# Run-in of the L2 attention heads: other spare products on TensorE

## The chip, the cores and the metric

The kernel runs on one core of a Trainium2 chip. The metric is the time of one execution on the device in microseconds (us); lower is better. Half a per cent of it is about 9.7 us.

## The reference, cut to what matters

A sequence of 2 x 1024 tokens with 256 features passes four layers, all in float32: L0 (cumulative-sum attention and a feed-forward), L1 (single-head attention and a feed-forward), L2 (16-head attention with heads of 16 features) and L3 (16 heads of 64 features, then an expert stage). The change touches the heads of L2 only:

```python
h = _sln(hidden, w, ln_g, ln_b, Wg, bg, Wb, bb)
qkv = (h @ Wqkv.T + bqkv).reshape(B, N, num_heads, hd, 3)
q = jnp.moveaxis(qkv[..., 0], 2, 1)
k = jnp.moveaxis(qkv[..., 1], 2, 1)
v = jnp.moveaxis(qkv[..., 2], 2, 1)
energy = jnp.einsum('bhqd,bhkd->bhqk', q, k)
att = jax.nn.softmax(energy, axis=-1) / D ** 0.5
out = jnp.einsum('bhqk,bhkd->bhqd', att, v)
```

With B = 2 and 16 heads there are 32 maps of 1024 x 1024 scores with an inner size of 16.

## The kernel before

The layers run one after the other as stages; a barrier of all engines stands between two. The stage of the L2 heads is `NarrowPairs`. It takes the 32 heads in 16 pairs; the two heads of a pair sit in the two halves of the 128 rows of the TensorE array (rows 0 to 63 and rows 64 to 127). Queries and keys are split into a high and a low part of the type fp32r and stacked, so that one product with 48 rows gives the three cross terms.

Scores are computed twice. First by query rows (`row`, L1756): two products of 48 x 128 weights and 512 columns fill a PSUM tile `rowb` of 128 x 1024 for each head, and VectorE takes the row maximum of it (L1824, tile `l2h_nm`). The maxima of a pair are turned and placed as two more rows of the stacked queries (the DMAs of `place_shift`). Then by keys (`score`, L1772): 50-row products give the shifted scores, already transposed; ScalarE takes the exponent (L1874, into `pT`), and `mix` (L1786) multiplies by the values. A mix uses all 128 rows and 32 columns of the array, four side by side. Its operands are plain float32, and each such product shows as two records in the trace.

`pe_program` is one hand-written order: for turns m = -2 to 16, steps k = 0 to 7, phases 0 and 1. In each phase come two `row` products of one head, each followed by a `score` product of the pair m on the other half of the array, and then `mix` products of two steps before. `ahead` says which rows are due: those of pair m + 1 (k below 4) or m + 2, so row maxima run twelve steps ahead of the scores. In the turns m below 0 there are no scores yet: the 12 steps with rows (8 of pair 0, 4 of pair 1), 24 phases, are the **run-in**. In it `ahead_of_scores` (L1763) puts spare products where the scores will stand later: 48 rows, 512 columns, in the half of the array that `row` does not use, into a `score` tile that nobody reads. Nothing waits for them, and they wait for nothing.

`row` waits with its first product for the maximum taken before from the same `rowb` half (semaphore `maxes`); VectorE waits for `rowsums`. Steps 0 and 1 of pair 0 (m = 0) have no mix, since a mix comes two steps behind. At the end of the stage `pe_out` (L2336) puts some ordinary float32 products of 128 x 128 weights and 256 columns between the last scores; they belong to the output projection.

Of the kernel before, what the change touches and what calls it, by code (L numbers as in the profile page):

```python
# [22 lines left out]
P = 128  # L23
# [4 lines left out]
C = 512  # L28
# [10 lines left out]
class Semaphores:  # L39


    def __init__(self, nc):
        self.nc, self.held = nc, []
# [1597 lines left out]
class NarrowPairs:  # L1641
# [8 lines left out]
    OUT = 5  # L1650

    def __init__(self, s, parts, V, out, ident, hd, vscale, tiles, pending, later):
        self.V, (self.out, self.sums), self.hd, self.vscale = V, out, hd, vscale
        self.mw = 32
        (self.K, self.Q), self.pending = tiles, pending
        self.Q = self.Q + [s.sb("Q3", [P, S], F32R)]
        self.vs = s.sb("vs", [P, self.SLOTS, 2, TB, self.mw])
        self.pT = s.sb("pT", [P, 4, 2, S])
        self.osb = s.sb("osb", [P, 2, C])
        self.nm = s.sb("nm", [P, 2, 2 * TB])  # L1660
        self.parts_nm = s.sb("nm_parts", [P, 4 * TB], F32R)
        self.shift = s.sb("shift", [P, 4 * TB])
        self.rowb = [s.ps(f"rowb{i}", (P, S)) for i in range(2)]
        self.score = [s.ps(f"score{i}") for i in range(3)]
        self.ob = s.ps("out")
        self.loaded = [s.sem(f"loaded{i}") for i in range(self.SLOTS)]
        self.stored = [s.sem(f"stored{i}") for i in range(2)]
        (self.constants, self.staged, self.rowsums, self.maxes, self.high, self.split, self.turned, self.shifted,
         self.scores, self.exps, self.mixed, self.ocopied) = (s.sem(n) for n in (
             "v_constants", "v_staged", "row_scores", "maxima", "maxima_hi", "maxima_lo", "maxima_turned",  # L1670
             "shift_in_stack", "scores", "exps", "mixed", "out_copied"))
        self.q, self.k = parts
        self.second_load, self.last_store, self.second_pair = later
# [73 lines left out]
    def pe_program(self, pe):  # L1747
        def row(m, t, h, c):
            u, r = m % self.SLOTS, 64 * h
            if c == 0:  # L1750
                if t == 0:
                    self.need(pe, self.loaded[u], (m // self.SLOTS + (u >= self.EARLY)) * 16 * self.LOADS)
                    if m == 1:
                        pe.wait_ge(self.second_pair, 16 * self.LOADS)
                self.need(pe, self.maxes, (TB * m + t) * 2 + h - 1)
            mm = pe.matmul(self.rowb[h][:, c * C:(c + 1) * C], self.Q[u][r:r + self.SPLIT, t * P:(t + 1) * P],  # L1756
                           self.K[u][r:r + self.SPLIT, c * C:(c + 1) * C], start=True, stop=True)
            if c == 1:
                mm.then_inc(self.rowsums, 1)

        def ahead_of_scores(t, h, c):
            r = 64 * h
            pe.matmul(self.score[2 - 2 * h][:, :], self.Q[0][r:r + self.SPLIT, t * P:(t + 1) * P],  # L1763
                      self.K[0][r:r + self.SPLIT, c * C:(c + 1) * C], start=True, stop=True)

        def score(m, k, h, c, place):
            u, r = m % self.SLOTS, 64 * h
            v = 4 * (TB * m + k) + place
            if k == 0 and place == 0:
                pe.wait_ge(self.shifted, 8 * 16 * (m + 1))  # L1770
            self.need(pe, self.exps, v - 2)
            pe.matmul(self.score[v % 3][:, :], self.K[u][r:r + self.SPLIT + 2, k * P:(k + 1) * P],  # L1772
                      self.Q[u][r:r + self.SPLIT + 2, c * C:(c + 1) * C], start=True, stop=True).then_inc(self.scores, 1)

        def mix(m, k, part):
            g = TB * m + k
            if part == 0:
                pe.wait_ge(self.exps, 4 * (g + 1))
            if k == 0 and part == 0:
                pe.wait_ge(self.staged, m + 1)  # L1780
                self.need(pe, self.ocopied, m)
            at, w = (part * C // 2, C // 2) if 0 < k < TB - 1 else (0, C)
            for h in range(2):
                for c in range(2):
                    r = self.mw * (2 * h + c)
                    mm = pe.matmul(self.ob[r:r + self.mw, at:at + w], self.vs[:, m % self.SLOTS, h, k, :],  # L1786
                                   self.pT[:, g % 4, h, c * C + at:c * C + at + w], start=k == 0, stop=k == TB - 1)
            if at + w == C:
                mm.then_inc(self.mixed, 1)

        for m in self.TURNS:
            for k in range(TB):
                mr, tr = self.ahead(m, k)
                for phase in range(2):
                    for c in range(2):
                        if self.there(mr):
                            row(mr, tr, phase, c)
                        if self.there(m):
                            score(m, k, *self.part(mr, phase, c))
                        elif m < 0 and self.there(mr):  # L1800
                            ahead_of_scores(tr, 1 - phase, c)
                    mine, kk = (m, k - self.LAG) if k >= self.LAG else (m - 1, k - self.LAG + TB)
                    if self.there(mine) and (phase == 0 or 0 < kk < TB - 1):
                        mix(mine, kk, phase)
                step = TB * (m - self.N + 2) + k - self.OUT
                if step == 0:
                    pe.wait_ge(self.maxes, 2 * TB * self.N)
                if 0 <= step < 2:
                    self.tokens.pe_out(pe, 0, self.rowb[0], 2 * step, 2 * step + 2)
                elif 2 <= step < 6:  # L1810
                    self.tokens.pe_out(pe, 1, self.rowb[1], step - 2, step - 1)
# [1481 lines left out]
```

## Time and profile before

| | us |
|---|---|
| median of 3 runs | 1941.92 (1938.81 to 1947.23) |
| the profiled execution | 1945.03 |
| its span on the core | 1943.3 |
| TensorE busy (share of the span) | 1768.1 (91%) |
| VectorE busy | 1471.1 (76%) |
| ScalarE busy | 1142.5 (59%) |
| GpSimd busy | 815.7 (42%) |

The heads of L2 run from 510.7 to about 882 us. A timeline row has its start, its length, engine, line, operation and tiles; rows of one kind that follow each other are merged (x2, x8), and lengths of neighbours on PE overlap, so the time that a product takes from the engine is read as the distance between starts. PE is the matmul, PEld the load of its weights. PEclk is the granted TensorE clock as a share of full speed: 0.50 is 1.2 GHz, 1.00 is 2.4 GHz.

### The profile page before, as it was taken

How to read it: one execution, taken by the hardware profiler on the slowest of the kernel's cores; microseconds unless marked ns; L12 is line 12 of the kernel's file. 1: busy time of each engine (PE TensorE's matmuls, PEld its weight loads, DVE VectorE, ACT ScalarE, POOL GpSimd, SP SyncE). 2: the span in 40 equal slices, each digit the busy share in tenths (PEclk: the TensorE clock that was granted, in tenths of full speed). 3: DMA queues.
4: the chain of work that ended last, by engine and by line, in shares of the span. 5: the costliest groups of instructions: out<-in, count | busy, mean ns of one | idle time of the engine just before them, and what ended most of it. 6: DMA issues, size and time to landing. Idle time of an engine off the chain costs nothing. (4 is left out here: it accounts for less than half of the span.)

```text
span 1943.3 us, 37413 instructions
## 1 busy us (share of the span) xinstructions
PE 1768.1 (91%) x14461; PEld 1169.6 (60%) x14461; DVE 1471.1 (76%) x2454; ACT 1142.5 (59%) x2029; POOL 815.7 (42%) x738
## 2 busy tenths in 40 slices
PE   7998999898799999998989599999999999882896
PEld 5766589697533333346767465566666666671885
DVE  5666745745779999986987688888888888467794
ACT  3332333533158888875567577777777777332663
POOL 3465620464130411002655545544555555105576
PEclk9999999999669999999999899999999999995888
DMA  5000000201523212213669854555456553308352
GB/s 161 1 1 28 1 14 1 66 1 45 187 60 98 59 41 54 53 30 120 203 203 281 218 120 107 120 124 117 113 124 160 143 141 88 109 12 252 95 141 44
DMA packets 196193, 191.28 MB, mean 98 GB/s; under 512 B 64496, under 2 KB 154352, under 8 KB 195760
## 3 DMA queue, kind: packets, MB, share of 16 engines
q1 hardware_dynamic: 192944, 184.69, 35.6%
q0 software_dynamic: 3072, 4.20, 1.2%
q8 instruction: 115, 1.88, 0.4%
q14 instruction: 62, 0.51, 0.1%
HBM read 121.20 MB, written 67.37 MB: 97 GB/s over the span
## 5 line engine op out<-in xcount | busy, mean ns | idle before, releaser
L1624 POOL TENSOR_SCALAR l3h_prob<-l3h_prob,l3h_inv 128x1024 f32<-128x1024 f32 x256 | 284.4, 1124 | 283.6 <-DVE l3h_inv L1584 283.6
L1824 DVE TENSOR_REDUCE l2h_nm<-l2h_rowb 128x1 f32<-128x1024 f32 x256 | 302.6, 1218 | 29.1 <-PE l2h_rowb L1756 28.7
L1577 DVE TENSOR_REDUCE l3h_nmax<-l3h_score 128x1 f32<-128x1024 f32 x256 | 309.6, 1215 | 12.1 <-PE l3h_score L1514 8.2
L1874 ACT ACTIVATE l2h_pT<-l2h_score 128x512 f32<-128x512 f32 x512 | 273.9, 597 | 51.2 <-PE l2h_score L1772 31.8
L1607 ACT ACTIVATE l3h_prob<-l3h_score,l3h_nmax 128x1024 f32<-128x1024 f32 x256 | 282.5, 1113 | 2.9 <-DVE l3h_nmax L1577 2.7
L1569 DVE COPY l3h_pT<-l3h_ring 128x512 f32<-128x512 f32 x256 | 176.2, 688 | 95.5 <-PE l3h_ring L1527 95.5
L1539 PE MATMUL l3h_out<-l3h_pT,l3h_vs 128*64 128x512 f32 x1024 | 247.3, 605 | 0.8 <-ACT l3h_osb L1600 0.8
L1571 ACT ACTIVATE l3h_pT<-l3h_ring 128x512 f32<-128x512 f32 x256 | 154.2, 602 | 138.8 <-PE l3h_ring L1527 138.8
L1527 PEld LDWEIGHTS l3h_ring<-ident,l3h_prob 64*128 64x128 f32 x4096 | 157.2, 138 | 129.0 <-POOL l3h_prob L1624 111.6
L1527 PE MATMUL l3h_ring<-ident,l3h_prob 64*128 64x64 f32 x4096 | 175.3, 225 | 9.7 <-POOL l3h_prob L1624 8.0
L1786 PE MATMUL l2h_out<-l2h_pT,l2h_vs 128*32 128x256 f32 (+1 forms) x1792 | 160.1, 431 | 0.0
L2701 POOL TENSOR_TENSOR l3qkv_lo<-l3qkv_full,l3qkv_hi 128x1024 fp32r<-128x1024 f32 x32 | 97.9, 3063 | 95.0 <-ACT l3qkv_hi L2598 95.0
L1756 PE MATMUL l2h_rowb<-l2K,l2Q 48*128 48x512 f32 x256 | 103.6, 502 | 11.5 <-PEq L69 7.7
L1514 PE MATMUL l3h_score<-k3first,q3first 64*128 64x512 f32 x768 | 106.6, 409 | 7.7 <-PEq L69 6.1
L1539 PEld LDWEIGHTS l3h_out<-l3h_pT,l3h_vs 128*64 128x64 f32 x1024 | 62.6, 136 | 84.6 <-issue 76.2
L1514 PE MATMUL l3h_score<-l3h_K,l3h_Q 64*128 64x512 f32 x768 | 105.7, 405 | 0.4
L1772 PE MATMUL l2h_score<-l2Q,l2K 50*128 50x512 f32 x256 | 99.3, 472 | 1.1 <-ACT l2h_pT L1874 0.5
L1299 POOL TENSOR_TENSOR l1mlp_y_lo<-l1mlp_y,l1mlp_y_hi 128x512 fp32r<-128x512 f32 x32 | 44.6, 1418 | 125.3 <-DVE l1mlp_y_hi L1411 125.3
L1756 PEld LDWEIGHTS l2h_rowb<-l2K,l2Q 48*128 48x128 f32 x256 | 45.3, 216 | 72.7 <-DVE l2h_nm L1824 57.6
L1786 PEld LDWEIGHTS l2h_out<-l2h_pT,l2h_vs 128*32 128x32 f32 x1792 | 35.9, 109 | 77.1 <-issue 47.5
L1514 PEld LDWEIGHTS l3h_score<-k3first,q3first 64*128 64x128 f32 x768 | 68.3, 188 | 20.8 <-issue 6.3
L1514 PEld LDWEIGHTS l3h_score<-l3h_K,l3h_Q 64*128 64x128 f32 x768 | 67.4, 186 | 13.1 <-ACT l3h_prob L1607 1.8
(484 smaller groups left out, 4288.8 us busy)
## 6 DMA issues: line engine op xcount, KB each, us to landing
q3first<-l_q SPq DMA_DIRECT2D x64, 256.0 KB, 4.3
l3h_Q<-l_q SPq DMA_DIRECT2D x64, 256.0 KB, 4.2
l_q<-l3qkv_hi SPq DMA_DIRECT2D x16, 512.0 KB, 5.0
l_q<-l3qkv_lo SPq DMA_DIRECT2D x16, 512.0 KB, 4.6
l_k<-l3qkv_hi SPq DMA_DIRECT2D x16, 512.0 KB, 4.3
l_k<-l3qkv_lo SPq DMA_DIRECT2D x16, 512.0 KB, 3.4
k3first<-l_k SPq DMA_DIRECT2D x64, 128.0 KB, 4.5
l3h_vs<-l_v SPq DMA_DIRECT2D x32, 256.0 KB, 2.8
```

Source lines behind the costliest of these rows:

```text
L1514: mm = pe.matmul(self.score[t % 2][:, c * C:(c + 1) * C], self.Q[u][r, x, t * P:(t + 1) * P], self.K[u][r, y, :], start=i == 0, stop=i == 2)
L1527: mm = pe.transpose(self.turn_bank(g, half)[:, kk * P // 2:(kk + 1) * P // 2], self.prob[r, g % 4, kk * P:(kk + 1) * P], self.ident[r, r])
L1539: mm = pe.matmul(self.ob[c * self.hd:(c + 1) * self.hd, :], self.vs[:, n % 2, kk, :], self.pT[:, n % 2, kk, c * C:(c + 1) * C], start=kk = ...
L1569: eng.tensor_copy(dst, src).then_inc(self.emptied_d, 1)
L1571: eng.activation(dst, src, ACT.Copy).then_inc(self.emptied_a, 1)
L1577: dve.tensor_reduce(self.nmax[:, g % 4:g % 4 + 1], self.score[g % 2][:, :], AX.X, ALU.max, negate=True).then_inc(self.maxes, 1)
L1607: act.activation(self.prob[:, q, :], self.score[g % 2][:, :], ACT.Exp, bias=self.nmax[:, q:q + 1], accum_out=self.total[:, q:q + 1]).then_ ...
L1624: pool.tensor_scalar(self.prob[:, q, :], self.prob[:, q, :], self.inv[:, q:q + 1], self.vscale, ALU.mult, ALU.mult).then_inc(self.scaled, 1)
L1756: mm = pe.matmul(self.rowb[h][:, c * C:(c + 1) * C], self.Q[u][r:r + self.SPLIT, t * P:(t + 1) * P], self.K[u][r:r + self.SPLIT, c * C:(c ...
L1786: mm = pe.matmul(self.ob[r:r + self.mw, at:at + w], self.vs[:, m % self.SLOTS, h, k, :], self.pT[:, g % 4, h, c * C + at:c * C + at + w], ...
L1824: dve.tensor_reduce(self.nm[:, mr % 2, at:at + 1], self.rowb[h][:, :], AX.X, ALU.max, negate=True).then_inc(self.maxes, 1)
L1874: act.activation(self.pT[:, g % 4, h, c * C:(c + 1) * C], self.score[v % 3][:, :], ACT.Exp).then_inc(self.exps, 1)
```

## The change

The spare products of the run-in are others. `ahead_of_scores` goes, and `spare` comes: the identity (128 x 128, float32) as weights, 256 columns of the tokens `X` as the moving operand, into the first 256 columns of `score[0]` and `score[1]`. They use all 128 rows and all 128 columns of the array, and plain float32 in place of fp32r. There were four spare products in a step, one after each `row` product; there are still four, but two behind each pair of `row` products. So the number stays at 48. The results are read by nobody, as before.

```diff
-        def ahead_of_scores(t, h, c):
-            r = 64 * h
-            pe.matmul(self.score[2 - 2 * h][:, :], self.Q[0][r:r + self.SPLIT, t * P:(t + 1) * P],
-                      self.K[0][r:r + self.SPLIT, c * C:(c + 1) * C], start=True, stop=True)
+        def spare(i):
+            pe.matmul(self.score[i][:, 0:2 * P], self.ident[:, :], self.tokens.X[:, i, :],
+                      start=True, stop=True)
@@
                             row(mr, tr, phase, c)
                         if self.there(m):
                             score(m, k, *self.part(mr, phase, c))
-                        elif m < 0 and self.there(mr):
-                            ahead_of_scores(tr, 1 - phase, c)
+                    if m < 0 and self.there(mr):
+                        for i in range(2):
+                            spare(i)
```

On TensorE (PE), at the start of the stage of the L2 heads, the order before is this (`l2h_rowb` is written by `row`, `l2h_score` by the spare products; one row of before is one product):

```order
L69 UNCONDITIONAL_BRANCH
L2062 UNCONDITIONAL_BRANCH
L1756 MATMUL l2h_rowb<-l2K,l2Q 128x512
L1763 MATMUL l2h_score<-l2K,l2Q 128x512
L1756 MATMUL l2h_rowb<-l2K,l2Q 128x512
L1763 MATMUL l2h_score<-l2K,l2Q 128x512
L1756 MATMUL l2h_rowb<-l2K,l2Q 128x512
L1763 MATMUL l2h_score<-l2K,l2Q 128x512
```

And this is what stands on the same engine at the same place with the change (x2 are two products in a row):

```order
L69 UNCONDITIONAL_BRANCH
L2062 UNCONDITIONAL_BRANCH
L1756 MATMUL l2h_rowb<-l2K,l2Q 128x512 x2
L1762 MATMUL l2h_score<-X,ident 128x256 x2
L1756 MATMUL l2h_rowb<-l2K,l2Q 128x512 x2
L1762 MATMUL l2h_score<-X,ident 128x256 x2
```

Row products of one half of the array no longer have a neighbour for the other half; each two of them are followed by two products that take the whole array. The other engines' instructions are the same, in the same order.

## Rows read from the trace of the kernel before

**Rows 1.** Page: busy share in 40 slices of the span, and the granted clock.

```profile
PE   7998999898799999998989599999999999882896
...
DVE  5666745745779999986987688888888888467794
...
PEclk9999999999669999999999899999999999995888
```

**Rows 2.** Stretches: us, busy and count of PE, PEld, DVE, ACT, POOL; PEclk; DMA share; GB/s.

```profile
511.00:541.00 30.00, 27.40 (x96) 12.09 (x96) 27.14 (x26) 0.00 (x0) 3.55 (x12) 0.50 0.66 201
547.00:566.00 19.00, 18.80 (x101) 6.54 (x100) 12.05 (x14) 10.15 (x20) 8.65 (x8) 0.50 0.01 1
570.00:575.00 5.00, 5.00 (x50) 1.94 (x43) 4.65 (x4) 4.39 (x10) 3.54 (x3) 1.00 0.82 152
```

**Rows 3.** Timeline of the run-in: its first product, one phase, the first real score.

```profile
510.76 0.76 PE L1756 MATMUL l2h_rowb<-l2K,l2Q 48*128 48x512 f32 x1 [7.73 <-PEq L69]
...
538.98 0.79 PE L1756 MATMUL l2h_rowb<-l2K,l2Q 48*128 48x512 f32 x1 [0.18 <-DVE l2h_nm L1824]
538.98 0.28 PEld L1763 LDWEIGHTS l2h_score<-l2K,l2Q 48*128 48x128 f32 x1
538.98 0.79 PE L1763 MATMUL l2h_score<-l2K,l2Q 48*128 48x512 f32 x1
...
540.24 2.36 DVE L1824 TENSOR_REDUCE l2h_nm<-l2h_rowb 128x1 f32<-128x1024 f32 x2 [0.17 <-PE l2h_rowb L1756]
...
541.52 0.79 PE L1772 MATMUL l2h_score<-l2Q,l2K 50*128 50x512 f32 x1
```

**Rows 4.** Timeline of PE: one phase at half clock, then the start of the next.

```profile
560.04 0.79 PE L1772 MATMUL l2h_score<-l2Q,l2K 50*128 50x512 f32 x1
560.63 0.62 PE L1756 MATMUL l2h_rowb<-q3first,k3first 48*128 48x512 f32 x1
...
561.19 1.08 PE L1786 MATMUL l2h_out<-l2h_pT,l2h_vs 128*32 128x256 f32 x8
562.20 0.79 PE L1756 MATMUL l2h_rowb<-q3first,k3first 48*128 48x512 f32 x1
```

**Rows 5.** Timeline of PE: the same at full clock.

```profile
588.69 0.64 PE L1786 MATMUL l2h_out<-l2h_pT,l2h_vs 128*32 128x256 f32 x8
589.26 0.49 PE L1756 MATMUL l2h_rowb<-q3first,l2h_Q 48*128 48x512 f32 x1
...
589.92 0.64 PE L1786 MATMUL l2h_out<-l2h_pT,l2h_vs 128*32 128x256 f32 x8
```

**Rows 6.** Timeline of PE at full clock: whole-array float32 products between half-array scores.

```profile
865.65 0.50 PE L1772 MATMUL l2h_score<-l2h_Q,q3first 50*128 50x512 f32 x2
866.08 1.13 PE L2336 MATMUL l2h_rowb<-carry,V 128*128 128x256 f32 x4
867.14 0.51 PE L1772 MATMUL l2h_score<-l2h_Q,q3first 50*128 50x512 f32 x2
```

**Rows 7.** Weight loads of whole-array float32 products of 512 columns at half clock.

```profile
466.05 0.34 PEld L2002 LDWEIGHTS l2qkv_bank<-l2qkv_norm_out,carry 128*128 128x128 f32 x1 [0.52 <-issue]
466.90 0.34 PEld L2002 LDWEIGHTS l2qkv_bank<-l2qkv_norm_out,carry 128*128 128x128 f32 x1 [0.52 <-issue]
```

**Rows 8.** VectorE once in each pair, behind the pair's last row maximum (pairs 1 to 3).

```profile
556.07 0.17 DVE L1831 CAST l2h_nm_parts<-l2h_nm 128x16 fp32r<-128x16 f32 x1
581.32 0.17 DVE L1831 CAST l2h_nm_parts<-l2h_nm 128x16 fp32r<-128x16 f32 x1
601.58 0.17 DVE L1831 CAST l2h_nm_parts<-l2h_nm 128x16 fp32r<-128x16 f32 x1
```

**Rows 9.** Stretches in which the clock rises, stays or falls elsewhere (columns as in Rows 2).

```profile
463.00:464.00 1.00, 0.54 (x3) 0.57 (x4) 0.97 (x5) 1.00 (x2) 0.00 (x0) 0.50 0.00 0
...
467.00:468.00 1.00, 1.00 (x3) 0.49 (x2) 0.00 (x0) 1.00 (x2) 1.00 (x1) 0.74 0.00 0
...
501.50:505.00 3.50, 1.53 (x13) 1.33 (x12) 2.28 (x5) 0.00 (x0) 0.00 (x0) 1.00 0.72 148
505.00:506.00 1.00, 0.00 (x0) 0.00 (x0) 0.00 (x0) 0.00 (x0) 0.00 (x0) 0.53 0.53 195
```

More of the change, by code:

```diff
@@ L1652, in __init__ @@
     def __init__(self, s, parts, V, out, ident, hd, vscale, tiles, pending, later):
-        self.V, (self.out, self.sums), self.hd, self.vscale = V, out, hd, vscale
+        self.V, (self.out, self.sums), self.ident, self.hd, self.vscale = V, out, ident, hd, vscale
         self.mw = 32
```

## The prediction

> **What bounds the kernel now.** I read the page's slices first. TensorE is busy nearly everywhere, but in slices 11 and 12 the granted clock falls to 0.6 [rows 1]. Those slices hold the start of the L2 heads, so next I read the stretches there. From 511 to 541 us, the run-in, PEclk is 0.50 (1.2 GHz), PE is busy 27.40 of 30 us and VectorE 27.14 of 30; from 547 to 566 us PE is busy 18.80 of 19 us and the clock is still 0.50; from 570 us it is 1.00 [rows 2]. Thus the place has two parts with different limits:
>
> In the run-in **VectorE** sets the pace in spite of the slow clock. A pair of row maxima takes 2.36 us, VectorE waits only 0.17 us before it, and the next row product waits for the maximum [rows 3]. The run-in lasts from 510.76 to 541.52 us: 30.76 us for 24 phases, 1.28 us a phase.
>
> Behind it **TensorE at half clock** sets the pace. A phase there is 1.15 us of row and score products and 1.01 us of mixes, 2.16 us (560.04 to 561.19 to 562.20) [rows 4]; at full clock it is 0.66 us (589.26 to 589.92) and 0.57 us (588.69 to 589.26) [rows 5].
>
> What the slow clock costs: a pair in steady state takes 601.58 - 581.32 = 20.26 us. From one such mark (behind the fourth step's maxima) to the next, the one before takes 581.32 - 556.07 = 25.25 us, 5.0 more [rows 8]. For the part before 556.07 us: the mark lies four steps behind the first score, 556.07 - 541.52 = 14.5 us; four steps are half of 20.26, and the mark comes about 1 us after them (the last maximum has to wait for its product), which makes 11.1 us in steady state. That is 3.4 us more. Together **8.4 us**: all that a perfect clock behind the run-in could give back. Of it I take 7.5, since the exponent table is still loaded by ScalarE at the first score.
>
> **The change, part by part.**
>
> *Removed:* 48 half-array spare products. Each ran in the other half of the array beside a row product, with the same start, 538.98 us [rows 3]. They took no time of their own: worth 0.
>
> *Added:* 48 whole-array float32 products, two in each phase. They can't run beside row products, for they need the rows of both halves. A float32 product of 512 columns is two records, and at half clock one follows the other by 0.85 us (466.05 to 466.90) [rows 7]; at 256 columns I take half, 0.43 us, so two products, four records, are 1.71 us. Passing from half-array to whole-array products and back has a price: at full clock four records stand between scores for 867.14 - 866.08 = 1.06 us [rows 6], 0.86 us of it streaming by half of 0.43 each, and 0.20 us the change-over. At half clock the mixes show a change-over of 1.01 - 0.86 = 0.15 us [rows 4] against 0.57 - 0.43 = 0.14 us at full [rows 5], so it grows little; I take 0.25 us. Bounds: 0.15 and 0.35.
>
> The row products alone: each two follow each other in the same half, as now; 1.15 us at half clock [rows 4], 0.66 us at full [rows 5]. I don't expect them to be quicker without a neighbour in the other half. Lower bounds are 1.00 and 0.43 us, if the change-over is counted only once (a pair of scores before the whole-array products takes 866.08 - 865.65 = 0.43 us [rows 6]).
>
> So a phase of the run-in is
>
> - at half clock 1.15 + 1.71 + 0.25 = **3.11 us** (2.86 to 3.2), against 1.28 now;
> - at full clock 0.66 + 1.06 = **1.72 us** (1.29 to 1.72), against 1.28 now.
>
> Either way TensorE becomes the bound of the run-in and VectorE, with 1.2 us of work a phase, waits. The cover that hid spare work (the other half of the array) is gone, and the four products a step lie on the path. Nothing else moves: no wait is added, the queues of the other engines hold the same instructions, and the loads of later pairs only get more time.
>
> The Trainium skill says the same of the change-over: "TensorEngine Tiling (Array Packing)", section "Key Properties", has a switch of the tiling mode drain the engine. By that rule each phase pays two drains that the present spare products, of the same mode as the rows, don't pay. The trace agrees, with the 0.20 us above.
>
> **Does the clock rise?** This decides the size. For it: whole-array products with little else bring it up within about 4 us (PE idle in part of 463 to 464 us, 0.74 in 467 to 468 us) [rows 9]. Against it: from 547 to 566 us TensorE is busy 99% [rows 2], 47% of it with mixes on all rows and columns and 53% with products on 96 to 98 rows [rows 4], and yet the clock stays at 0.50 for 19 us. In the new run-in the whole-array products hold 1.96 of 3.11 us, 63%, but the remaining 37% are row products on 48 of 128 rows with nothing beside them. By rows in use times streaming time, the new mix has 1.71 + 0.375 x 0.85 = 2.03 us in 3.11, or 0.65; the stretch that stayed cold has 0.86 + 0.77 x 0.86 = 1.52 us in 2.16, or 0.70; the present run-in has 0.77 x 0.86 in 1.28, or 0.51. So the new run-in is more active than the old one, but no more than a stretch that stayed slow for 19 us. I take it that the clock stays low through the run-in, with little certainty.
>
> **Sum of the forecast (case A).** 24 x 3.11 = 74.6 us in place of 30.8: +43.9 us (68.6 to 76.8 by the bounds: +38 to +46). Behind the run-in the same slow stretch of about 19 us as now follows, as the products there are unchanged: 0, give or take 5. The profiled execution would go from 1945.0 to 1989; it lies 3.1 us above the median, and from the median 1941.9 it is **1986 us**, own range 1979 to 1993.
>
> **Rivals.**
>
> *B, the clock rises early and stays.* Two phases at half clock, the rest full: 24 x 1.72 + 2 x 1.39 = 44.1 us, +13.3; the 7.5 us behind it are won: +5.8, 1948 us. The skill's page "TensorE: Matmul & The Clock Gate", Part 1, speaks for a rise: there the throttled clock is the default state and sustained matmul activity releases it. The rows at 467 us agree with it; those at 547 to 566 us don't, busy as the engine is.
>
> *C, it rises early and falls again.* In steps 0 and 1 of pair 0 there are no mixes, and at full clock the engine has 0.66 us of half-array work in each 1.28 us. At 501.5 to 505 us it was busy 1.53 of 3.5 us and the clock fell [rows 9]. Then most of the 7.5 us are lost again: +12, 1954 us.
>
> *D, it rises late,* after some twelve phases: 10.6 + 12 x 1.39 - 7.5 = +19.8, 1962 us.
>
> *E, not slower.* The clock rises at once and the change-overs are hidden, so that a phase at full clock is 0.43 + 0.86 = 1.29 us, and VectorE stays the bound. The run-in then grows by 3.4 us only (two phases at 2.86, the rest 0.01 each), and 7.5 are won: -4, 1938 us. It decides where a phase at full clock falls below 1.45 us, since 24 x 0.17 + 3.4 = 7.5. The 1.06 us of rows 6 speaks against it. Even without any cost the gain would end at 8.4 us, below half a per cent.
>
> **How the numbers follow.** A 0.50, B 0.20, C 0.13, D 0.12, E 0.03, others 0.02. About 0.5% (9.7 us) can be told from no change here. A, C and D are slower by more: 0.75; B and E within it: 0.23; faster by more: 0.02. The predicted time is A's, 1986 us. B must be partly in the range, since A, C and D alone hold 0.75: 1947 to 1993 us.
>
> **What would show it.** In the timeline of the changed kernel the first real score (now at 541.52 us) should come at about 585 us, with PEclk 0.50 in all stretches before, four records of the identity product 0.43 us apart in each phase, and VectorE idle near 1.9 us before each maximum. If PEclk is 1.00 from some point on, the phases from there are to be 1.72 us long, and the case is B, C or D by when it rises and whether 541 to 548 us' counterpart keeps it. I am wrong in the sizing if a phase at half clock is not near 3.1 us, and wrong in the main step if the clock rises among row products on 48 rows.

## The result

The changed kernel takes 1986.2 us (median of 6 executions, 1982.78 to 1990.55), the kernel before 1946.3 us (6 executions, 1938.81 to 1951.84). The ratio is 1.0206 with a 95% interval of 1.0182 to 1.0230: 2% slower, 40 us. The median of the kernel before is now 4.4 us above the 1941.9 of the forecast, which came from its first three executions. The profiled execution of the changed kernel has a span of 1988.8 us, against 1943.3.

The answers to [rows 1] are these lines of the page after: the busy share in 40 slices and the granted clock, each slice now 49.7 us.

```profile
PE   7998999899899999998989789999999999892886
...
DVE  6676646656347999996888688888888888556896
...
PEclk9999999999557999999999899999999999995798
```

TensorE is busier than before in slices 11 and 12 (89 where there was 79), VectorE less (34 where there was 77), and the clock in them went from 66 to 55, with a 7 in the slice behind. More work, no more speed.

The stretches of the changed kernel that answer to [rows 2] (us, busy and count of PE, PEld, DVE, ACT, POOL; PEclk; DMA share; GB/s):

```profile
509.00:584.00 75.00, 75.00 (x144) 39.89 (x144) 29.95 (x27) 0.00 (x0) 3.54 (x12) 0.50 0.32 89
584.40:622.50 38.10, 37.12 (x189) 14.02 (x188) 23.34 (x22) 21.51 (x39) 15.96 (x12) 0.50 0.09 22
625.00:630.00 5.00, 4.99 (x44) 1.84 (x40) 4.64 (x5) 4.18 (x9) 0.00 (x0) 1.00 0.11 25
```

The run-in is over 75 us long now. PE is busy in all of the first stretch, VectorE in 30 of its 75 us, and the clock is 0.50 throughout. The bound has gone from VectorE to TensorE. The timeline of the run-in's end, answering to [rows 3]:

```profile
579.27 2.07 PE L1762 MATMUL l2h_score<-X,ident 128*128 128x256 f32 x4
579.38 1.23 DVE L1824 TENSOR_REDUCE l2h_nm<-l2h_rowb 128x1 f32<-128x1024 f32 x1 [1.93 <-PE l2h_rowb L1756]
...
581.27 1.22 PE L1756 MATMUL l2h_rowb<-l2K,l2Q 48*128 48x512 f32 x2
...
582.42 2.07 PE L1762 MATMUL l2h_score<-X,ident 128*128 128x256 f32 x4
...
584.43 0.79 PE L1771 MATMUL l2h_score<-l2Q,l2K 50*128 50x512 f32 x1
```

One phase is 1.15 us of row products (581.27 to 582.42) and 2.01 us of spare ones (582.42 to 584.43), 3.16 us in all, and VectorE waits 1.93 us before its maximum where it had waited 0.17 for a pair of them. The first row product comes at 508.77 us, the first real score at 584.43: 75.7 us for 24 phases, 44.9 more than before.

Behind it the slow stretch is a little longer than it was. The marks of [rows 8] are now at

```profile
598.99 0.17 DVE L1831 CAST l2h_nm_parts<-l2h_nm 128x16 fp32r<-128x16 f32 x1
630.04 0.17 DVE L1831 CAST l2h_nm_parts<-l2h_nm 128x16 fp32r<-128x16 f32 x1
650.34 0.17 DVE L1831 CAST l2h_nm_parts<-l2h_nm 128x16 fp32r<-128x16 f32 x1
```

and 630.04 - 584.43 = 45.6 us from the first score to the second of them, against 581.32 - 541.52 = 39.8. The last pair has the steady 20.3 us. The balance of the profiled executions: start of the stage 2.0 us earlier, run-in +44.9, slow stretch +5.8, the rest of the program about -3, span +45.5. The medians are 40 us apart; a single execution of either kernel lies some microseconds off, and the profiled one of the changed kernel was the longest of its six.

### The profile page after: what moved, and what is told of

Same layout as the page of the kernel before. It is cut to its first block and busy times, and to the rows that moved or that the text cites. A ratio compares the mean times of both kernels' runs of the same rounds, so it can differ in the third digit from the quotient of the medians.

```text
span 1988.8 us, 37509 instructions
## 1 busy us (share of the span) xinstructions
PE 1818.5 (91%) x14509; PEld 1200.7 (60%) x14509; DVE 1475.0 (74%) x2454; ACT 1141.3 (57%) x2029; POOL 809.7 (41%) x738
## 5 line engine op out<-in xcount | busy, mean ns | idle before, releaser
L1514 PEld LDWEIGHTS l3h_score<-l3h_K,l3h_Q 64*128 64x128 f32 x768 | 68.0, 186 | 12.8 <-ACT l3h_prob L1607 1.8
```

Source lines behind the costliest of these rows:

```text
L1514: mm = pe.matmul(self.score[t % 2][:, c * C:(c + 1) * C], self.Q[u][r, x, t * P:(t + 1) * P], self.K[u][r, y, :], start=i == 0, stop=i == 2)
```

## The experiments

Each kernel is told by its difference to the kernel before or the changed one. Only spare products differ. A time without a number of executions is that of a single one. In one of the comparisons below, 23 executions of the kernel before reached from 1931.5 to 1954.9 us around a median of 1945.6, so a single time can be off by some 10 us, and the readings rest on the traces. "Theory" and "rival" are those of the expectation shown.

**Spare products taken away.** Of before, without the two lines that call `ahead_of_scores`:

```diff
-                        elif m < 0 and self.there(mr):
-                            ahead_of_scores(tr, 1 - phase, c)
```

> The run-in without any spare product: only the two row products of each phase are left on TensorE. The changed kernel's extra time is put down to spare products that have the array to themselves; the spare products of before ran beside the rows and should have cost nothing. Theory: VectorE still sets the pace, 24 phases of 1.28 us, first row product to first real score 30.8 us, PEclk 0.50, total as before, 1942 to 1947 us. Rival (the spare products of before already did something for the clock): the slow stretch behind the run-in gets longer than 25 us by over 10 us, total 1950 or more.

Measured: 1951.9 us, beside 1954.2 for the kernel before on the same chip. The run-in's stretch:

```profile
511.00:541.00 30.00, 26.30 (x49) 10.94 (x45) 27.66 (x27) 0.00 (x0) 3.03 (x11) 0.50 0.68 200
```

And two pairs of maxima in its timeline:

```profile
537.18 2.36 DVE L1822 TENSOR_REDUCE l2h_nm<-l2h_rowb 128x1 f32<-128x1024 f32 x2 [0.18 <-PE l2h_rowb L1756]
...
539.72 2.36 DVE L1822 TENSOR_REDUCE l2h_nm<-l2h_rowb 128x1 f32<-128x1024 f32 x2 [0.18 <-PE l2h_rowb L1756]
```

VectorE's pairs of maxima are 2.54 us apart (537.18 to 539.72), two phases of 1.27 us: as with the spare products. These had cost no time in a phase, and the clock came back 25 us after the first score with them and without. The first score itself came later than expected, 32.8 us after the first row product (510.25 to 543.01) and not 30.8: it waited 1.22 us for the transfer of the shifts. Whether that is chance of this one execution isn't shown.

**One whole-array product a phase.** Of the changed kernel:

```diff
                     if m < 0 and self.there(mr):
-                        for i in range(2):
-                            spare(i)
+                        spare(phase)
```

> One whole-array spare product in each phase in place of two. Theory (streaming of the product, 0.43 us a record at half clock, carries the cost, and a change-over of about 0.3 us is paid once a phase): a phase of 1.15 + 0.86 + 0.29 = 2.30 us at PEclk 0.50, run-in 55 us against 75.7 with two, total about 1966 us. Rival (the change between half-array and whole-array products carries the cost, whatever the number): a phase of 2.9 us or more, total 1980.

Measured: 1969.8 us. The timeline of PE:

```profile
540.05 1.22 PE L1756 MATMUL l2h_rowb<-l2K,l2Q 48*128 48x512 f32 x2
541.20 1.22 PE L1762 MATMUL l2h_score<-X,ident 128*128 128x256 f32 x2
542.35 1.22 PE L1756 MATMUL l2h_rowb<-l2K,l2Q 48*128 48x512 f32 x2
```

A phase is 2.30 us, 0.85 less than with two. The product costs its streaming, two records of 0.43 us. The theory holds for the phase and for the run-in (55.2 us), and the total lies 4 us above its 1966 us; the rival (2.9 us whatever the number) is out.

**Two more change-overs a phase.** Of the changed kernel, the same 48 products in another order:

```diff
                             score(m, k, *self.part(mr, phase, c))
-                    if m < 0 and self.there(mr):
-                        for i in range(2):
-                            spare(i)
+                        elif m < 0 and self.there(mr):
+                            spare(c)
```

> The changed kernel with its two spare products of a phase placed one behind each row product instead of both behind the second: the same 48 products, but two changes more in a phase between half-array and whole-array products. It measures the change-over by itself. Theory (about 0.3 us for a change there and back at half clock): a phase of 3.15 + 0.3 = 3.45 us, run-in 83 us, total about 7 us above the changed kernel. Rival (the change-over costs nothing, the rest of the 3.15 us is weight loading of the products themselves): 3.15 us a phase.

Measured: 1995.3 us, and a timeline of PE of

```profile
538.32 0.79 PE L1756 MATMUL l2h_rowb<-l2K,l2Q 48*128 48x512 f32 x1
539.04 1.22 PE L1762 MATMUL l2h_score<-X,ident 128*128 128x256 f32 x2
540.19 0.79 PE L1756 MATMUL l2h_rowb<-l2K,l2Q 48*128 48x512 f32 x1
540.91 1.22 PE L1762 MATMUL l2h_score<-X,ident 128*128 128x256 f32 x2
542.06 0.79 PE L1756 MATMUL l2h_rowb<-l2K,l2Q 48*128 48x512 f32 x1
```

A phase is 3.74 us (538.32 to 542.06), not the 3.45 expected: two changes more cost 0.59 us, so **one change is 0.29 us at half clock**, in either direction. A row product alone takes 0.72 us, 0.43 of it streaming; a spare product 1.15 us, 0.86 of it streaming. With that the changed kernel's phase comes out: 4 x 0.43 + 2 x 0.43 + 2 x 0.29 = 3.16 us. I had put the way into the whole-array products too low, at 0.25 us in the prediction, and in the expectation I had put both ways together at 0.3 us. The run-in grew by 14 us against the changed kernel, the total by 9 against its median: the clock came back 10 us after the first score here and 38 us after it there.

**Both kinds of spare products.** Of the changed kernel, with `ahead_of_scores` put back beside the rows (called `beside`):

```diff
                         if self.there(m):
                             score(m, k, *self.part(mr, phase, c))
+                        elif m < 0 and self.there(mr):
+                            beside(tr, 1 - phase, c)
                     if m < 0 and self.there(mr):
                         for i in range(2):
                             spare(i)
```

> The changed kernel with the half-array spare products of before put back beside the row products, in addition to the two whole-array ones. Theory (the clock stays low because the row products leave over half of the array idle for 1.15 of 3.15 us): the first phases take 3.15 us, as now, then PEclk goes to 1.00 within the run-in, and phases take 1.72 us; run-in 42 to 60 us, total 1950 to 1970. Rival (products with the identity as weights, nearly all zeros, don't count for the clock): PEclk 0.50 for all of the run-in, 3.15 us a phase, total 1986.

Measured: 1959.5 us. Stretches:

```profile
513.00:528.00 15.00, 15.00 (x40) 8.23 (x40) 6.12 (x5) 0.00 (x0) 2.60 (x10) 0.50 0.63 199
530.00:561.00 31.00, 31.00 (x145) 17.55 (x144) 22.14 (x22) 0.00 (x0) 0.00 (x0) 1.00 0.38 103
561.00:567.00 6.00, 4.66 (x22) 2.30 (x20) 5.01 (x5) 5.23 (x10) 0.00 (x0) 1.00 0.00 0
568.00:570.00 2.00, 2.00 (x12) 0.83 (x6) 0.25 (x1) 0.23 (x2) 0.00 (x0) 0.50 0.00 0
```

This is the run that tells most, and the theory holds. The products added take no time of their own (3.15 us a phase at half clock, 514.98 to 518.13), yet the clock rises within the run-in, near 529 us, and from then on a phase is

```profile
531.84 0.50 PE L1756 MATMUL l2h_rowb<-l2K,l2Q 48*128 48x512 f32 x1
...
532.51 1.13 PE L1762 MATMUL l2h_score<-X,ident 128*128 128x256 f32 x4
533.57 0.50 PE L1756 MATMUL l2h_rowb<-l2K,l2Q 48*128 48x512 f32 x1
```

1.73 us long, 0.67 and 1.06. So the clock stayed low in the changed kernel although PE was busy 75 of 75 us, and what it lacked was the products beside the rows, in the other half of the array. Behind the first score, in the steps without mixes, the clock falls again, but only from 567.0 to 570.5 us. To see whether the rise is regular, the same kernel was timed:

> The kernel with both kinds of spare products again, now timed: whether the clock rises within the run-in every time or did so once. Theory: in every execution it rises somewhere in the run-in, the total lies between 1945 and 1972 us by when, the clock of each execution is above the 0.93 of the changed kernel. Rival (it was chance): some executions at 1984 to 1991 us with 0.93.

Measured: 1955.0 us median of 10 executions (1945.25 to 1961.95), ratio to before 1.0048 (1.0026 to 1.0071). The clock of the executions is 0.945 to 0.956; with the changed kernel it is 0.929 to 0.934 in all six. By these clocks and times it rises each time; two of the eleven executions were profiled and show it. In the new profile it rose at about 515 us, in the second phase:

```profile
514.00:515.00 1.00, 1.00 (x5) 0.35 (x5) 0.00 (x0) 0.00 (x0) 0.37 (x2) 0.50 1.04 193
515.00:516.00 1.00, 1.00 (x4) 0.79 (x4) 0.98 (x1) 0.00 (x0) 0.00 (x0) 0.77 0.95 201
516.00:517.00 1.00, 1.00 (x7) 0.41 (x6) 0.26 (x2) 0.00 (x0) 0.00 (x0) 1.00 0.68 70
```

Even so the kernel is no faster than before. The run-in takes 43.6 us (510.61 to 554.16), 12.8 more than before, and from the first score to the second of the marks of [rows 8] (here at 587.16 us) it takes 33.0 us against 39.8, 6.8 less: a run-in of 1.73 us a phase costs more than the clock gives back.

**Other weights.** Of the changed kernel:

```diff
-            pe.matmul(self.score[i][:, 0:2 * P], self.ident[:, :], self.tokens.X[:, i, :],
+            pe.matmul(self.score[i][:, 0:2 * P], self.tokens.X[:, 2 + i, 0:P], self.tokens.X[:, i, :],
```

> The changed kernel with 128 columns of the tokens as weights of the spare products in place of the identity, so that nearly all weights are other than zero. Theory (the weights' values don't matter; it is the half-array rows without a neighbour): 3.15 us a phase, PEclk 0.50 through the run-in, total 1980 to 1991. Rival (zeros in the weights kept the clock low): it rises within the run-in, total below 1972.

Measured: 1983.0 us, PEclk 0.50 through the run-in, and on PE

```profile
540.70 1.22 PE L1756 MATMUL l2h_rowb<-l2K,l2Q 48*128 48x512 f32 x2
541.85 2.07 PE L1762 MATMUL l2h_score<-X 128*128 128x256 f32 x4
543.85 1.22 PE L1756 MATMUL l2h_rowb<-l2K,l2Q 48*128 48x512 f32 x2
```

a phase of 3.15 us. The theory holds: the zeros of the identity are not what kept the clock low.

**Starting with a full clock.** Of the changed kernel, 14 products at the end of TensorE's program of the stage before, in the time in which it waits for the barrier:

```diff
+            for i in range(14):
+                pe.matmul(bank[0][:, 0:2 * P], g["ident"][:, :], X[:, i % 2, :], start=True, stop=True)
```

> The changed kernel with 14 more identity products at the end of the stage before, in the 7 us in which TensorE waits for the barrier, so that the run-in starts at full clock. Theory: at PEclk 1.00 a phase takes 0.66 + 1.06 = 1.72 us, the run-in 41 us if the clock holds; total 1944 to 1956 by whether the clock also holds in the two steps without mixes. Rival (the clock falls in the run-in even when it starts full): phases go back to 3.15 us, total 1975 to 1986.

Measured: 1993.0 us. The theory fell. The rival has the phase right; the time lies above its 1975 to 1986 us. PE's timeline, and two stretches of it:

```profile
503.47 6.21 PE L2024 MATMUL l2qkv_bank<-X,ident 128*128 128x256 f32 x28
511.20 0.69 PE L1756 MATMUL l2h_rowb<-l2K,l2Q 48*128 48x512 f32 x2 [1.53 <-PEq L69]
511.82 1.26 PE L1762 MATMUL l2h_score<-X,ident 128*128 128x256 f32 x4
513.01 1.22 PE L1756 MATMUL l2h_rowb<-l2K,l2Q 48*128 48x512 f32 x2
```

```profile
512.00:513.00 1.00, 1.00 (x4) 0.50 (x4) 1.00 (x1) 0.00 (x0) 1.00 (x3) 0.85 0.66 236
513.00:514.00 1.00, 1.00 (x3) 0.50 (x2) 0.16 (x1) 0.00 (x0) 1.00 (x6) 0.50 0.69 223
```

The stage starts at full clock, but PE had stood still for 1.5 us at the barrier, and within the first phase the clock falls. From 515 to 580 us it is 0.50 with PE busy 65 of 65 us. So once low, it did not come back in a run-in of this make, here and in the changed kernel. Whether the standstill or the row products without neighbours took it down, this run doesn't tell apart.

The same 14 products ahead of the run-in of the kernel before:

> The kernel before with 14 whole-array products in the wait for the barrier ahead of the stage, and its own half-array spare products in the run-in. In the two-product run-in that began full the clock fell after the first phase; here the row products have a neighbour in the other half, but at full clock TensorE would be busy with them only 0.66 of 1.28 us. Theory: PEclk is 1.00 for the first microseconds and falls to 0.50 within about 5 us, total as before (within 5 us). Rival (half-array pairs keep a clock that is already full): PEclk 1.00 up to the first real score and behind it, the slow stretch is gone, 7 to 8 us faster than before.

Measured: 1947.8 us. PEclk is 0.92 from 511 to 512 us and 0.50 from 512 to 540; it comes back at about 566 us, as in the kernel before. The theory holds, no gain. Here too PE had stood still at the barrier, for 2.09 us, so the run doesn't show that half-array pairs alone lose a full clock.

**Keeping it.** Three kernels tried to beat both. The first has the 14 products, `beside`, and one whole-array product a phase:

```diff
+                        elif m < 0 and self.there(mr):
+                            beside(tr, 1 - phase, c)
                     if m < 0 and self.there(mr):
-                        for i in range(2):
-                            spare(i)
+                        spare(phase)
```

> Three things at once: 14 products in the wait for the barrier, half-array spare products beside the rows, one whole-array spare product a phase. Theory: PEclk 1.00 from the start of the run-in to its end, a phase of 0.66 + 0.64 = 1.30 us, run-in 31 to 32 us; then in the two steps without mixes the clock falls once, as it did behind the run-in with both kinds of spares, and comes back within some microseconds; 2 to 6 us faster than before. Rival (one whole-array product in 1.3 us does not hold the clock): 2.30 us a phase, 24 us slower.

Measured: 1969.5 us. The theory fell: PE stood still for 1.98 us at the barrier, the first phase is at full clock, then it is lost (PEclk 0.50 from 510 to 602 us), and each phase takes 2.30 us. The next adds, in the two steps of the first pair without mixes, one whole-array product a phase:

```diff
+                    if m == 0 and k < self.LAG:
+                        pe.matmul(self.ob[:, 0:2 * P], self.ident[:, :], self.tokens.X[:, phase, :],
+                                  start=True, stop=True)
```

> The same, and one whole-array spare product in each phase of the two steps of the first pair that have no mixes. Theory: the clock stays at 1.00 from the stage's start on, the slow stretch of 25 us behind the run-in is gone, first real score to the mark behind the second pair's maxima 31 to 33 us in place of 39.8; 5 to 8 us faster than before, a ratio of 0.996 to 0.998. Rival (the fillers delay the scores as much as the clock gives back): no faster than without them.

Measured: five executions of 1940.6, 1965.9, 1973.8, 1974.7 and 1975.3 us, with a clock of 0.955, 0.941, 0.933, 0.933 and 0.935; the kernel before had a median of 1949.7 us beside them. Only the first is faster than that, by 9 us where 5 to 8 were forecast. It was the one profiled: the clock survived the barrier, after a standstill of 2.07 us, and a phase was 1.29 us (509.04 to 510.33). By their clocks and times it was lost in three; the one of 1965.9 us lies between. Up to the first score the program is that of the kernel above, where it was lost after 1.98 us: the length of the standstill alone doesn't decide.

With 16 products in the wait and one spare product more in the first step (the edit is against the kernel just told):

```diff
-                        spare(phase)
+                        for i in range(2 if m == -2 and k == 4 and phase == 1 else 1):
+                            spare((phase + i) % 2)
```

> With 14 products in the barrier's wait the clock of the run-in stayed full in a part of the executions only, since TensorE still stood still for 2.0 us at the barrier: full means 1941 us, lost means 1974. Here 16 products, so that the gap is about 1.2 us, and one more whole-array spare product in the first step, while VectorE is still on its first two maxima. Theory (the gap decides): the clock holds in most executions, which are at 0.994 to 0.998 of the kernel before; few or none near 1974. Rival (one whole-array product a phase holds it only by chance): executions at 1970 to 1976 in about half of the cases.

Measured: 1945.1 us median of 12, of which one at 1970.0 (clock 0.937) and one at 1957.4; ratio 0.9997 (0.9969 to 1.0026) without the one at 1970.0. PE waits 1.31 us at the barrier there. By their clocks and times it holds through the run-in in most executions, as the theory said, but the ratio of 0.994 to 0.998 was missed. The profile shows one reason: in the steps without mixes the clock was lost after all, in spite of their whole-array products, from 546.1 to 556.4 us.

```profile
546.00:548.00 2.00, 1.92 (x5) 0.84 (x5) 0.81 (x1) 1.49 (x4) 0.00 (x0) 0.55 0.00 0
...
556.00:558.00 2.00, 2.00 (x18) 0.90 (x14) 1.33 (x2) 1.69 (x4) 0.00 (x0) 0.89 0.00 0
```

And with 17 in the wait and two spare products in each of the first four phases:

```diff
-                        for i in range(2 if m == -2 and k == 4 and phase == 1 else 1):
+                        for i in range(2 if m == -2 and k < 6 else 1):
```

> As that one, with 17 products in the wait (a gap of about 0.8 us, or the barrier later by some tenths) and two whole-array spare products in each of the first four phases, 1.72 us each at full clock: 1.8 us more work in the run-in. Theory: the clock holds in all executions, ratio 0.996 to 0.999. Rival as there: some executions near 1974.

Measured: 1941.3 us median of 12 (1938.27 to 1947.39), before 1945.6 of 23; ratio 0.9990 (0.9965 to 1.0014). No execution lies near 1974 us, and all clocks are 0.950 to 0.957; the ratio lies inside the forecast of 0.996 to 0.999, at its edge. The stretches:

```profile
511.00:543.00 32.00, 32.00 (x151) 15.44 (x149) 28.44 (x27) 0.00 (x0) 3.48 (x12) 1.00 0.68 197
543.00:550.00 7.00, 6.47 (x30) 2.94 (x29) 5.72 (x5) 5.52 (x9) 0.00 (x0) 1.00 0.34 51
550.00:560.00 10.00, 9.87 (x90) 3.66 (x88) 9.40 (x12) 8.40 (x16) 3.65 (x2) 1.00 0.01 2
```

The clock is 1.00 from the first product on (PE stood still for 0.40 us only), and the slow stretch is gone. From the first row product to the first score it takes 543.4 - 510.7 = 32.7 us (before 30.8), from there to the last copy of the heads' outputs 874.5 - 543.4 = 331.1 us (before 879.9 - 541.5 = 338.4): +1.9 and -7.3, 5.4 us won in the stage. In the total this can't be told from no change: the interval reaches from 7 us faster to 3 us slower.

## Why the prediction was right

*What carries the sum.* 24 phases of 3.11 us in place of 1.28 were predicted, 3.15 in place of 1.28 measured (75.66 us by 24); +43.9 against +44.9 us for the run-in in the profiled executions. Point by point: the removed products were worth 0 (run without them: 1.27 us a phase); the row products kept their 1.15 us; four records cost 1.71 us, as one product less takes off 0.85. The change-over was mis-sized: I took 0.25 us behind the 0.30 contained in the row products' 1.15; it is 0.29 each way. I let the 0.20 us of full clock grow little because the change-over of the mixes hardly does (0.14 to 0.15 us); that of the spare products grows to 0.29. That is the 0.04 us a phase, or 1 us, by which the run-in is longer.

*The nearness of the total is luck.* The forecast was 44 us on top of 1941.9; measured are 39.9 us on top of 1946.3. Two misses of some 4 us cancel to 1986.2 against 1986. As the run-in alone costs 44.9 us in the profile, the rest of the program must have been about 5 us shorter by the medians (an estimate: 39.9 - 44.9), which "0, give or take 5" just covers.

*The clock.* The step that decided the size, that it stays at 0.50, held in the profile and, by their clocks and times, in the other five executions, but it was a half-and-half judgement, and that it came out is in part luck. The argument for it (row products alone leave the greater part of the array idle) fits the runs: with a neighbour in the other half it rises, with other weights it doesn't. Whether it is the rows, or something else that comes with two products at a time, is not told apart.

*Behind the run-in.* "0, give or take 5" was +5.8 in the profile. The stretch from the first score to the rise of the clock was

- 25 us before, and 25 without spare products;
- 23 with one whole-array product a phase;
- 25 in the kernel before and 23 in the changed one with 14 products in the wait;
- 39 with these 14, products beside the rows and one whole-array product a phase;
- 10 with the split order, 10 with token weights, and 38 in the changed kernel.

The instructions of that stretch are the same in all nine; what ran before it isn't. The last two differ only in the values of the weights, had the same phases and PEclk 0.50 in the run-in, and still stand at 10 and 38. So from single profiles the +5.8 us can't be put down to the change. What sets the length stays open.

*The rivals.* B was sized rightly by its phase (1.72 predicted, 1.73 measured in the run with both kinds), but in the changed kernel it doesn't occur. Its sum of +5.8 us stands against 9 us there by the ratio. C doesn't occur in the changed kernel either. In the other it has its mechanism right and its price wrong: in both of that kernel's profiles the clock fell in the steps without mixes, but for 3.4 us only, and 6.8 of the 8.4 us came back, where C had lost most of 7.5. That its 1954 us lies near the 1955.0 us of that kernel is chance. E, not slower, is out: the change-over costs 0.2 us at full clock too (1.06 us for four records in the run with both kinds), as [rows 6] had shown.

## What to carry to other kernels

Spare work is free only as long as it uses what the real work leaves idle: a product on the other half of the array cost nothing here, a whole-array product cost its full streaming and, at half clock, 0.29 us for each change of shape. Work out first the most that a full clock could give back (8.4 us here) and set it against the price of the filler when the clock does not rise. And it was cheaper to keep a clock than to win it back: products put into a wait for a barrier cost nothing that could be seen (the stage began at 510.7 us with 17 of them, 510.8 before), those in the run-in did. But even the kernel that kept the clock in 12 of 12 executions can't be told from the one before.

## What the runs showed of the hardware

TensorE busy 75 of 75 us kept a granted clock of 0.50, with whole-array float32 products in 2.01 of each 3.16 us and 48-row products in the rest. The same engine time, with 48-row products in the other half beside them, brought it to 1.00 in the run-in, 17.7 us after its start in one profile and 4.7 us in the other, and in all ten timed executions as their clocks show. A busy engine is not enough.

A change between 48-row and whole-array products took 0.29 us at half clock, either way, and 0.20 us at full clock.

One kernel can have two courses: with 14 products ahead of the barrier and a standstill of about 2 us, one execution in five kept the clock, three took some 34 us more, and nothing in the program differs. With a standstill of 0.40 us and a denser start it was kept 12 times in 12; which of the two does it, no run tells apart.
